# The first two blocks of each expert layer: early weights, rows chosen by 0/1 matrices, and a shift moved to VectorE, in a four-layer tower

## The chip, the cores and the metric

The kernel runs on 1 core of one Trainium2 chip, in float32. The metric is the device time of one execution in microseconds (us): the median of 3 runs.

## The reference, cut to what matters

Four layers run one after the other on 16 x 36 = 576 tokens of width 256. The change touches the mixtures of experts of layers 0, 2 and 3, called ffn0, ffn2 and ffn3 here. ffn0 sends each token to one of 8 experts, ffn2 to two of 8, ffn3 to two of 7.

```python
def _L0_ffn_ref(x, rms_w, gate_w, W1, b1, W2, b2):
    ms = jnp.mean(x * x, axis=-1, keepdims=True)
    xn = x * jax.lax.rsqrt(ms + EPS) * rms_w
    logits = jnp.einsum('btd,ed->bte', xn, gate_w)
    scores = jax.nn.softmax(logits, axis=-1)
    top1_idx = jnp.argmax(scores, axis=-1)
    top1_score = jnp.max(scores, axis=-1)
    out = jnp.zeros_like(xn)
    for e in range(E):
        h = jax.nn.silu(jnp.einsum('btd,df->btf', xn, W1[e]) + b1[e])
        ye = jnp.einsum('btf,fd->btd', h, W2[e]) + b2[e]
        out = jnp.where((top1_idx == e)[..., None], ye, out)
    return out * top1_score[..., None]
```

In ffn2 and ffn3 an expert is `silu(t @ a) * (t @ c) @ b`, the two chosen experts are summed with their weights, and one shared expert of the same form is added for every token. Between these stand recurrences (attn0, attn1, attn2, attn3) and a dense mixture (ffn1).

## The kernel before, in words

**An expert layer.** The normalized rows of the 576 tokens lie in `XH`, in five tiles of 128 tokens (the last has 64). TensorE transposes them, multiplies with the gate weights (`gate_logits`), VectorE finds the largest logits (`gates`), TensorE counts how many tokens each expert has ahead of each token (`ranks`), and VectorE turns that into a row number for each token (`places`). The rows of an expert fill whole blocks of 128 rows. The number of blocks is fixed, for the worst case: 12 in ffn0, 16 in ffn2, 15 in ffn3; `eid` says whose block each is. GpSimd scatters the rows of `XH` into the DRAM buffer `x_slots` (`dispatch`: 5 indirect DMAs in ffn0, 10 in ffn2 and ffn3). Then SyncE (SP) loads the blocks' rows and weights, TensorE multiplies, the result goes to `y_slots` in DRAM, and at the end GpSimd gathers it back per token (`collect`, with VectorE's `collect_tile`).

**The loop over blocks (`routed`).** Two weight buffers, each in two halves of about 1 MB. For block b, TensorE runs `up` of half 0, the `down` of half 1 of block b-1, the two transposes of the rows of block b+1, `up` of half 1, `down` of half 0. So a block is 24 products and 2 transposes in ffn0, 28 and 2 in ffn2 and ffn3. SP's program for block b (`emit` in `expert_blocks`) waits until the buffer's half is read (`downd`), and issues in this order: the rows of block b+2, half 0 of its weights, half 1, and then the finished rows of block b. All of these go through SP's one queue, in the order of the program.

**Which waits stand ahead of a layer.** SP waits for `eid_ready` before it loads any weights, and for all scatters (`scattered`) before it loads any rows.

**The shared expert** (`shared`) of ffn2 runs whole ahead of the blocks, in two halves of the tokens (384 and 192) with 3 steps each; that of ffn3 (6 steps per half) runs one half ahead of the blocks and one behind them. On VectorE, `weights` stands between `places` and `shared`.

**The shift b2 of ffn0** is added ahead of the blocks: TensorE transposes the gate weights `comb` and multiplies with `b20_s`, VectorE adds that to H (`side_tiles`). ScalarE copies each block's result to `y_s` (`y_copy`).

**keep_warm(n)** issues n turns of four bf16 products of 512 columns that nobody reads; `keep_warm(n, root=r)` then waits for a norm's variance and issues five more. They stand in TensorE's own order: what follows waits for them.

## Time and profile before

| | |
|---|---|
| runs | 862.98, 857.13, 854.99 us, median 857.13 |
| the profiled execution | 852.33 us, its span 850.5 us |
| TensorE busy | 768.8 us (90%) |
| mean granted TensorE clock | 0.979 |
| DMA moved | 139.45 MB, mean 164 GB/s |

All times in the rows further down are us from the start of that span. ffn0's blocks run from 121.34 to 212.5, ffn2's from 503.01 to 628.1, ffn3's from 711.08 to 829.5. In a timeline row, the first number is the start, the second the length; the bracket at its end is the idle time of that engine before it and what ended it. A float32 product shows as two records, so x48 is 24 products.

### The profile page before, as it was taken

To read this page: it belongs to the slowest core of one execution; us is meant where nothing else is said; L and a number is where in the kernel's file an instruction comes from. 1 tells how busy PE (TensorE), PEld (TensorE's weight loads), DVE (VectorE), ACT (ScalarE), POOL (GpSimd) and SP (SyncE) were. 2 spreads that over 40 slices of the span, in tenths; PEclk is the share of its full clock that TensorE was granted. 3 is DMA by queue.
4 is the path that set the end of the run, shared out by engine and by line. 5 is a ranking of instruction groups with operands and counts; after the bars stand their busy time and mean duration, and the time that the engine had idled before them with its cause. 6 is when DMAs were issued, how large, how long until landed. Compare 5 with 4: busy or idle time off the path is not lost.

```text
span 850.5 us, 12638 instructions
## 1 busy us (share of the span) xinstructions
PE 768.8 (90%) x4364; PEld 596.2 (70%) x4431; DVE 337.5 (40%) x949; ACT 254.6 (30%) x590; POOL 133.6 (16%) x101
## 2 busy tenths in 40 slices
PE   9999869999976679898988899999999989999996
PEld 6687449889543345674754579999965547999895
DVE  2215630000499957576758421111117731111113
ACT  1233124444353331563592222222210112222121
POOL 2000010000239940023050210000022040000004
PEclk9999889999999999999999799999999989999999
DMA  9700058996155502000000349999951062999962
GB/s 330 276 2 1 9 230 282 322 297 219 34 153 143 151 1 111 1 2 0 1 0 1 110 168 306 314 328 307 331 199 30 1 265 76 312 329 307 304 218 89
DMA packets 39842, 139.45 MB, mean 164 GB/s; under 512 B 5760, under 2 KB 20544, under 8 KB 28160
## 3 DMA queue, kind: packets, MB, share of 16 engines
q1 hardware_dynamic: 37568, 133.12, 46.7%
q0 software_dynamic: 2240, 5.90, 2.0%
q8 instruction: 18, 0.29, 0.2%
q14 instruction: 16, 0.13, 0.1%
HBM read 127.64 MB, written 11.35 MB: 163 GB/s over the span
## 4 chain that ended last, share of the span: by engine, by line
PE 59%; DVE 14%; issue 10%; DMA 8%; POOL 4%; ACT 3%; SPq 0%; DVEq 0%; POOLq 0%; ACTq 0%
PE PS L430 57%; DMA arena<-w_moe 4%; DVE arena L1680 4%; POOL arena L1281 2%; PE PS L487 1%; DVE stats L1362 1%; DMA arena<-x_slots 1%; PE PS L453 1%; DMA x_slots<-XH,posu 1%; DMA arena<-y_slots,posu 1%; POOL arena L1307 1%; DVE arena L1806 1%; DMA arena<-bc_scratch 1%; POOL arena L1294 1%; ACT XT L948 1%
## 5 line engine op out<-in xcount | busy, mean ns | idle before, releaser
L430 PE MATMUL PS<-arena 128*128 128x128 f32 (+4 forms) x2508 | 377.9, 310 | 12.1 <-DMA arena<-w_moe 3.1
L430 PEld LDWEIGHTS PS<-arena 128*128 128x128 f32 (+1 forms) x2508 | 334.7, 192 | 43.8 <-issue 13.4
L430 PE MATMUL PS<-warm 128*128 128x512 bf16 (+1 forms) x434 | 113.7, 379 | 7.8 <-DVE rs L1346 2.5
L1506 DVE TENSOR_TENSOR arena<-arena,PS 128x384 f32<-128x384 f32 (+1 forms) x62 | 30.2, 487 | 199.5 <-ACT arena L986 199.5
L430 PEld LDWEIGHTS PS<-warm 128*128 128x128 bf16 x501 | 49.7, 102 | 60.5 <-issue 7.1
L1281 POOL DMA_INDIRECT arena<-y_slots,posu x25 | 24.0, 961 | 381.7 <-DMA y_slots<-arena 375.0
L986 ACT ACTIVATE arena<-PS 128x384 f32<-128x384 f32 x62 | 30.4, 490 | 165.1 <-PE PS L430 165.1
L1294 POOL TENSOR_TENSOR arena<-arena 128x1152 f32<-128x1152 f32 x16 | 56.3, 3521 | 30.3 <-DVE arena L1680 30.3
L1518 DVE SCALAR_TENSOR_TENSOR H<-arena,wgt,H 128x256 f32<-128x256 f32 (+1 forms) x25 | 11.9, 477 | 120.6 <-DMA arena<-y_slots,posu 120.2
L430 PE MATMUL PS<-arena,ident 128*128 128x512 f32 (+1 forms) x128 | 38.0, 440 | 21.5 <-POOL arena L1294 21.5
L1270 POOL DMA_INDIRECT x_slots<-XH,posu x25 | 24.1, 964 | 172.5 <-DVE posu L1466 165.8
L430 PEld LDWEIGHTS PS<-arena,ident 128*128 128x128 f32 x128 | 20.5, 190 | 39.4 <-POOL arena L1294 24.1
L430 PE MATMUL PS<-XT,wsh 128*128 128x384 f32 (+1 forms) x144 | 43.5, 451 | 0.5 <-ACT arena L999 0.5
L1680 DVE TENSOR_TENSOR_SCAN arena<-PS,arena 128x576 f32<-128x576 f32 x32 | 41.6, 1340 | 0.0
L991 ACT ACTIVATE arena<-PS,arena 128x128 f32<-128x128 f32 x96 | 27.4, 367 | 43.1 <-PE PS L430 43.1
L430 PE MATMUL PS<-arena,wrnn_s 128*128 128x128 f32 (+1 forms) x280 | 36.7, 281 | 0.7
L430 PEld LDWEIGHTS PS<-arena,wrnn_s 128*128 128x128 f32 x280 | 33.8, 191 | 4.7 <-ACT arena L1052 3.9
L938 ACT ACTIVATE dev<-rs 128x5 f32<-128x5 f32 x19 | 4.1, 215 | 110.4 <-DVE rs L1346 110.4
L430 PEld LDWEIGHTS PS<-XT,wsh 128*128 128x128 f32 x144 | 28.0, 209 | 13.0 <-issue 5.5
L1113 ACT ACTIVATE PS<-arena 128x560 f32<-128x560 f32 x32 | 23.3, 731 | 35.5 <-DVE arena L1680 35.5
L430 PE MATMUL PS<-arena,wsh 128*128 128x384 f32 (+1 forms) x72 | 24.0, 460 | 9.7 <-DVE arena L1494 9.7
L999 ACT ACTIVATE arena<-PS 128x256 f32<-128x256 f32 x43 | 16.5, 383 | 38.5 <-PE PS L430 38.5
(262 smaller groups left out, 759.8 us busy)
## 6 DMA issues: line engine op xcount, KB each, us to landing
arena<-w_moe SPq DMA_DIRECT2D x31, 1152.0 KB, 6.5
arena<-w_moe SPq DMA_DIRECT2D x31, 1024.0 KB, 5.6
arena<-w_moe SPq DMA_DIRECT2D x24, 1026.0 KB, 6.1
arena<-bc_scratch SPq DMA_DIRECT2D x32, 288.0 KB, 3.8
arena<-x_slots SPq DMA_DIRECT2D x43, 128.0 KB, 2.5
y_slots<-arena SPq DMA_DIRECT2D x43, 128.0 KB, 5.2
wsh<-w_sh SPq DMA_DIRECT2D x1, 2176.0 KB, 8.5
wl_s<-w_l SPq DMA_DIRECT2D x1, 2048.0 KB, 13.1
```

Of the source, the lines that this page charges most:

```text
L430: return nc.tensor.matmul(out_, l, r, start=start, stop=stop, skip_group_check=True)
L453: last = nc.tensor.transpose(PS[:, j // 2, at:at + n_], XH[0:n_, j, 128 * d:128 * (d + 1)], ident[0:n_, 0:n_])
L986: nc.scalar.activation(sg_s[x][:, 0:3 * SB], PS[:, 2 * x, 0:3 * SB], ACT.Silu)\
L991: last = nc.scalar.activation(hid_b[x][:, SB * c:SB * (c + 1)], PS[:, 2 * x, SB * c:SB * (c + 1)], ACT.Silu, bias=wbuf[p][:, o_ + c:o_ + c ...
L999: nc.scalar.activation(y_s[p], PS[:, 4 + p, 0:D], ACT.Copy).then_inc(sem("y_sb"), 1)
L1113: nc.scalar.activation(inner(dA[d]), inner(dl[:, d, :]), ACT.Exp, scale=A_s[:, d, bass.ds(n, 1)])\
L1270: pool.indirect_dma_start(x_slots, bass.IndirectOffsetOnAxis(ap=posu[0:TILE_N[j], k, j:j + 1], axis=0), tile(XH, j), None).then_inc(sem("s ...
L1281: pool.indirect_dma_start(Yg[0:TILE_N[j], k, j * D:(j + 1) * D], None, y_slots[0:SB * NBLK[name], :], bass.IndirectOffsetOnAxis(ap=posu[0: ...
L1294: nc.gpsimd.tensor_tensor(hC[:, n % 2, :, :], hs_[:, n % 2, :, :], bcC[:, n:n + 1, :].to_broadcast([128, KD, T]), ALU.mult)\
L1506: ins = v.tensor_tensor(hid_b[x][:, 0:full], sg_s[x][:, 0:full], PS[:, 2 * x + 1, 0:full], ALU.mult)
L1518: link(v.scalar_tensor_tensor(tile(H, j), Yg[0:TILE_N[j], k, j * D:(j + 1) * D], wgt[0:TILE_N[j], k, j:j + 1], tile(H, j), ALU.mult, ALU.add))
L1680: v.tensor_tensor_scan(hs_[:, n % 2, d], dA[d], dBx[:, n % 2, d], 0.0, ALU.mult, ALU.add)\
```

## The change

1. **Blocks and experts.** Block e is the first 128 tokens of expert e; the blocks behind these hold what an expert has beyond 128. The numbers of blocks stay 12, 16 and 15. So blocks 0 and 1 always are experts 0 and 1, and SP issues their weights (`begin`) without `eid_ready`: in ffn0 when the products of the patches are done, in ffn2 and ffn3 when the recurrence ahead of them has read its last operands.
2. **Rows of blocks 0 and 1 in ffn0 and ffn2.** VectorE makes a 0/1 matrix per block (`chosen_rows`, five instructions of 128x128) and TensorE multiplies `XH` with it (`x_chosen`, ten products in place of a block's two transposes). In ffn3 the rows still come from `x_slots`.
3. **SP's order for block 0** in ffn0 and ffn2: half 0, half 1, then the wait for `scattered`, the rows of block 2, the finished rows.
4. **b2 of ffn0**: no products and no addition ahead of the blocks. SP loads the expert's row of b2 to 128 partitions for every block (`shift_in`), and VectorE adds it where ScalarE copied before (`shifted_rows`).
5. **gate_logits** multiplies the same eight gate columns twelve times over (96 columns), in all four layers that have gates; only the first eight are read.
6. **ffn2's shared expert**: one half ahead of the blocks, one behind them, as in ffn3. After it comes the same `keep_warm(21, root=18)`. The load of ffn3's shared weights now waits for it.
7. **VectorE's order** in ffn2 and ffn3: `places`, `shared`, `side_tiles`, then `weights`.
8. Four idle products ahead of the first `down` of the shared expert, seven ahead of attn1's last products.

```diff
@@ expert_blocks, on SP
-                def emit(b, hb, p, last=False):
+                def shift_in(e, p):
+                    if name == "ffn0":
+                        sp.dma_start(b2_s[p], b2_moe0[bass.ds(e, 1), :].to_broadcast([128, D])).then_inc(sem(f"b2{p}"), 16)
+
+                def emit(b, hb, p, last=False, first=False):
                     if not last:
                         e = expert_of(b + 2)
                         sp.wait_ge(sem("downd"), 2 * b + (2 * at + 1))
-                        rows_in(b + 2, p)
+                        if not first:
+                            rows_in(b + 2, p)
                         half(e, p, 0)
                         sp.wait_ge(sem("downd"), 2 * b + (2 * at + 2))
                         half(e, p, 1)
+                        if first:
+                            sp.wait_ge(sem("scattered"), 16 * SCAT[s])
+                            rows_in(b + 2, p)
                     rows_out(b, p)
-
-                sp.wait_ge(sem("eid_ready"), s + 1)
-                for b in range(2):
-                    e = expert_of(b)
-                    for x in range(2):
-                        half(e, b, x)
+                    if not last:
+                        shift_in(e, p)
+
+                def begin():
+                    for b in range(2):
+                        for x in range(2):
+                            half(b, b, x)
+                        shift_in(b, b)
@@ gate_logits, on TensorE
-                        last = mm(PS[0:TT, 3, E * j:E * (j + 1)], XT[:, k, TT * j:TT * (j + 1)],
-                                  gatew[:, GATES[name], k, :], k == 0, k == KD - 1)
+                        last = mm(PS[0:TT, 3, LG * j:LG * (j + 1)].rearrange("p (r e) -> p r e", e=E),
+                                  XT[:, k, TT * j:TT * (j + 1)],
+                                  gatew[:, GATES[name], k, None, :].to_broadcast([128, LG // E, E]), k == 0, k == KD - 1)
@@ routed, on TensorE
+                def x_chosen(b):
+
+                    pe.wait_ge(sem("one_hot"), 2 * ONE_HOT.index(name) + b + 1)
+                    for d in range(KD):
+                        for j in range(NT):
+                            last = mm(PS[:, 7 - b, SB * d:SB * (d + 1)], tile(XH, j)[:, 128 * d:128 * (d + 1)],
+                                      one_hot[b][0:TILE_N[j], j, :], j == 0, j == NT - 1)
                     last.then_inc(sem("xt_t"), 1)
@@ TensorE's program
+            idle_products(7)
             pe.wait_ge(sem("ys_ready"), 1)
@@
-            shared("ffn2", [128] * CS, ranked=True)
+            shared("ffn2", [128] * CS, (0,), ranked=True)
             routed("ffn2")
+            pe.wait_ge(sem("y_sb"), BLK0["ffn2"] + NBLK["ffn2"] + 2)
+            shared("ffn2", [128] * CS, (1,))
 
 
             keep_warm(21, root=18)
@@ VectorE
+            def chosen_rows(name, b):
+
+                if b == 0:
+                    dve.wait_ge(sem("xt_t"), BLK0[name]) if BLK0[name] else None
+                for j in range(NT):
+                    ins = v.tensor_scalar(one_hot[b][0:TILE_N[j], j, :], tri[0:TILE_N[j], 4, :], cnt[0:TILE_N[j], b, j:j + 1],
+                                          mks[0:TILE_N[j], b, j:j + 1], ALU.is_equal, ALU.mult)
+            def shifted_rows(b, hb, p):
+                dve.wait_ge(sem("downd"), 2 * b + 2)
+                dve.wait_ge(sem(f"y{p}"), 16 * hb + 16)
+                dve.wait_ge(sem(f"b2{p}"), 16 * hb + 16)
+                v.tensor_tensor(y_s[p], PS[:, 4 + p, 0:D], b2_s[p], ALU.add).then_inc(sem("y_sb"), 1)
```

How this moves instructions, at three places. The first is SP's program around block 0 of ffn0. `w_moe` are weights, `x_slots` the rows in, `y_slots` the rows out, `b_moe` the row of b2. Before, from the rows of blocks 0 and 1 to the end of `emit` for block 0:

```order
L359 DMA arena<-x_slots 128x256 x2
L350 TENSOR_LOAD eid
L350 ISA x2
L359 DMA arena<-x_slots 128x256
L356 ISA
L356 DMA arena<-w_moe 128x2052
L356 ISA
L356 DMA arena<-w_moe 128x2052
L363 DMA y_slots<-arena 128x256
```

Now, the same `emit`:

```order
L361 ISA
L361 DMA arena<-w_moe 128x2052
L361 ISA
L361 DMA arena<-w_moe 128x2052
L364 DMA arena<-x_slots 128x256
L368 DMA y_slots<-arena 128x256
L372 ISA
L372 DMA arena<-b_moe 128x256
```

The rows of block 2 have moved from ahead of its two halves of weights to behind both, and a load of b2 has come in behind the finished rows.

The second is TensorE's program in ffn0 from the ranks to the first products of block 0. `warm` are idle products, `ident,comb` and `b_s,combT` the shift, `ident,arena` the transposes of a block's rows. Before:

```order
L439 UNCONDITIONAL_BRANCH
L430 MATMUL PS<-warm 128x512 x4
L439 REGISTER_ALU
L439 COMPARE_AND_BRANCH
L707 MATMUL PS<-ident,comb 8x128 x4
L707 MATMUL PS<-ident,comb 8x64
L430 MATMUL PS<-b_s,combT 128x256 x4
L430 MATMUL PS<-b_s,combT 64x256
L439 UNCONDITIONAL_BRANCH
L430 MATMUL PS<-warm 128x512 x4
L439 REGISTER_ALU
L439 COMPARE_AND_BRANCH
L487 MATMUL PS<-ident,arena 128x128 x2
L430 MATMUL PS<-arena 128x128 x8
L487 MATMUL PS<-ident,arena 128x128 x2
L430 MATMUL PS<-arena 128x128 x8
```

Now (`arena,XH` are the products with the 0/1 matrices):

```order
L478 UNCONDITIONAL_BRANCH
L469 MATMUL PS<-warm 128x512 x4
L478 REGISTER_ALU
L478 COMPARE_AND_BRANCH
L469 MATMUL PS<-arena,XH 128x128 x10
L469 MATMUL PS<-arena 128x128 x8
L469 MATMUL PS<-arena,XH 128x128 x10
L469 MATMUL PS<-arena 128x128 x8
L469 MATMUL PS<-arena 128x256 x4
```

The shift and its idle products are gone, the three turns of idle products behind the ranks have stayed, and ten products stand where two transposes stood, twice.

The third is TensorE's program at the end of ffn2's blocks. Before:

```order
L430 MATMUL PS<-arena 128x128 x12
L430 MATMUL PS<-arena 128x256 x3
L430 MATMUL PS<-arena 128x128 x10
L430 MATMUL PS<-arena 128x256 x6
L439 UNCONDITIONAL_BRANCH
L430 MATMUL PS<-warm 128x512 x4
```

Now (`XT,wsh` and `arena,wsh` are the shared expert, `ident,YT` the transposes of its result):

```order
L469 MATMUL PS<-arena 128x128 x12
L469 MATMUL PS<-arena 128x256 x3
L469 MATMUL PS<-arena 128x128 x10
L469 MATMUL PS<-arena 128x256 x6
L469 MATMUL PS<-XT,wsh 128x192 x8
L469 MATMUL PS<-arena,wsh 128x192 x2
L469 MATMUL PS<-XT,wsh 128x192 x4
L469 MATMUL PS<-arena,wsh 128x192 x4
L604 MATMUL PS<-ident,YT 128x128 x2
L604 MATMUL PS<-ident,YT 64x128 x2
L478 UNCONDITIONAL_BRANCH
L469 MATMUL PS<-warm 128x512 x4
```

The second half of the shared expert stands between the last block and the 21 turns of idle products (L439 before, L478 now), which are the same.

## Rows read from the trace of the kernel before

**Rows 1.** The page, part 4: shares of the chain that ended last, by engine.
```profile
PE 59%; DVE 14%; issue 10%; DMA 8%; POOL 4%; ACT 3%; SPq 0%; DVEq 0%; POOLq 0%; ACTq 0%
```

**Rows 2.** The chain of waits around ffn0's start: start, length, what.
```profile
109.81 6.80 DMA x_slots<-XH,posu
116.62 3.18 DMA arena<-x_slots
121.34 3.75 PE PS L430 x16
```

**Rows 3.** Timeline of PE in ffn0: ranks, first transposes, one block.
```profile
99.54 1.45 PE L430 MATMUL PS<-mks,tri 128*128 128x40 f32 x6
...
119.85 0.69 PE L487 MATMUL PS<-ident,arena 128*128 128x128 f32 x2 [5.14 <-DMA arena<-x_slots]
...
132.51 7.19 PE L430 MATMUL PS<-arena 128*128 128x128 f32 x48
```

**Rows 4.** Timeline of DVE: a 128x128 instruction; places and weights in ffn2.
```profile
227.18 0.47 DVE L1632 TENSOR_SCALAR arena<-ident,colv 128x128 f32<-128x128 f32 x2
...
478.41 0.20 DVE L1437 COPY cnt<-PS 128x40 f32<-128x40 f32 x1 [2.48 <-PE PS L430]
...
481.77 0.23 DVE L1417 TENSOR_TENSOR gk<-mks,ge 128x40 f32<-128x40 f32 x1
...
483.86 1.02 DVE L1494 TENSOR_TENSOR arena<-arena,PS 128x384 f32<-128x384 f32 x2
```

**Rows 5.** Stretches: PE, PEld, DVE, ACT, POOL busy, granted clock, DMA share, GB/s.
```profile
97.10:99.50 2.40, 2.40 (x9) 0.71 (x6) 2.13 (x20) 0.52 (x1) 0.00 (x0) 0.66 0.01 3
101.00:105.30 4.30, 3.64 (x9) 1.53 (x11) 3.76 (x21) 0.00 (x0) 0.76 (x1) 0.57 0.00 0
121.30:125.20 3.90, 3.86 (x18) 3.89 (x19) 0.00 (x0) 1.26 (x2) 0.00 (x0) 0.50 0.00 0
473.30:477.60 4.30, 4.30 (x10) 2.42 (x10) 2.29 (x21) 1.52 (x2) 0.00 (x0) 0.60 0.00 0
487.20:491.40 4.20, 4.20 (x10) 2.29 (x9) 0.00 (x0) 0.00 (x0) 3.18 (x4) 0.62 1.02 426
```

**Rows 6.** More stretches, same columns: a block, attn1's end, ffn1's logits, ffn3.
```profile
146.80:154.00 7.20, 7.20 (x51) 6.69 (x50) 0.00 (x0) 3.18 (x11) 0.00 (x0) 1.00 0.98 334
205.00:212.00 7.00, 7.00 (x44) 6.43 (x44) 0.00 (x0) 2.67 (x9) 0.00 (x0) 1.00 0.09 28
312.20:318.60 6.40, 6.40 (x21) 4.62 (x22) 2.99 (x7) 0.00 (x0) 0.00 (x0) 0.73 0.00 0
333.00:340.40 7.40, 7.33 (x46) 6.43 (x47) 4.49 (x30) 1.53 (x3) 0.00 (x0) 1.00 0.00 1
677.10:681.40 4.30, 4.30 (x11) 2.38 (x11) 2.29 (x21) 1.52 (x2) 0.00 (x0) 0.62 0.00 0
```

**Rows 7.** SP's DMAs to y_slots, 132.9 to 134: block 0's, from issue to landing.
```profile
DMA to landing us min/median/max: 5.5/5.5/5.5
```

**Rows 8.** The page, part 6: DMA issues, size, median us to landing.
```profile
arena<-x_slots SPq DMA_DIRECT2D x43, 128.0 KB, 2.5
```

**Rows 9.** Timeline of PE in ffn2: wait, first block, last turns, next transposes.
```profile
484.47 2.93 PE L430 MATMUL PS<-arena,wsh 128*128 128x384 f32 x4 [3.41 <-DVE arena L1494]
...
503.01 2.92 PE L430 MATMUL PS<-arena 128*128 128x128 f32 x24 [0.56 <-ACT arena L975]
...
628.17 18.08 PE L430 MATMUL PS<-warm 128*128 128x512 bf16 x63
...
648.73 0.44 PE L453 MATMUL PS<-ident,XH 128*128 128x128 f32 x2 [0.27 <-DVE XH L1372]
```

**Rows 10.** Timeline of PE in ffn3: the wait, and the shared half at the end.
```profile
688.30 2.87 PE L430 MATMUL PS<-arena,wsh 128*128 128x384 f32 x4 [3.41 <-DVE arena L1494]
...
710.13 0.38 PE L487 MATMUL PS<-ident,arena 128*128 128x128 f32 x2
...
829.93 2.87 PE L430 MATMUL PS<-XT,wsh 128*128 128x192 f32 x16 [0.47 <-ACT arena L999]
```

## What the change does to the time, predicted

> **What bounds the kernel now.** I read the chain of waits first: TensorE carries 59% of it, and what is left comes in pieces between long runs of products [rows 1]. So a change pays only where TensorE waits, or where it works at the lower of its two clocks. I then went through the timeline of TensorE around the three layers of blocks, through VectorE's timeline for what it waits for there, and through a table of stretches for the granted clock and the DMA share.
>
> In ffn0 the end of the start-up is set by a path through memory. The last scatter lands 6.80 us after its start at 109.81, the rows take 3.18 us more, and the first products of block 0 start at 121.34 [rows 2]. TensorE has idled 5.14 us by then, and the clock is 0.50, so 1.2 GHz, up to 125.2 [rows 3, 5]. After that TensorE works without a break: 24 products, 4096 columns, in 7.19 us [rows 3], some 1.7 ns a column (128 columns 0.213 us), with a DMA share of 0.98 beside it [rows 6]. So in the blocks TensorE and the transfers are near a tie.
>
> In ffn2 and ffn3 the shared expert covers the scatter. What stands open is the 3.41 us in which TensorE waits for VectorE (`places`, then `weights`) [rows 4, 9, 10], and half clock ahead of it and behind it: 0.60 and 0.62 in ffn2, 0.62 in ffn3 [rows 5, 6].
>
> **The change part by part.** Sums are made against the profiled execution (852.33 us, 4.8 below the median 857.13), and the difference is carried over to the median.
>
> *a. ffn0, start.* Ranks start at 99.54 as now, as they wait for VectorE. They took 1.45 us at half clock; I take 0.73, the wide logits having kept the clock (c). Counts and offsets to the first 0/1 matrix are about six small steps of 0.2 us; the matrix is five instructions of 128x128 at 0.235 us or less [rows 4], about 1.1 us: ready at 102.6. The three turns of idle products, still ahead in TensorE's order, end at about 102.9. Ten products of 0.213 us give 105.0, ScalarE's copy 0.8: first product at 105.85 and not 121.34. **-15.5.** Weights are long there.
>
> *b. ffn0, block 1's rows* in ten products and not two transposes: eight more of 0.213. **+1.7.** Its matrix, made behind `places`, is ready at about 106, and TensorE asks at 107.5.
>
> *c. ffn0, block 2's rows.* Now SP issues them behind `downd` of block 0's second half, which falls inside block 1, and TensorE wants them right after that same `down`. Nothing hides the transfer, and it stands behind half 1 of the weights in the queue. The nearest row is the store of block 0's result, issued in just that place behind the same half: 5.5 us to landing [rows 7]. With 0.45 us for SP's two issues, TensorE waits **+5.95**. Behind this wait `up`, `down` and all later blocks queue. Bounds: 2.5 us, the median of such rows with little ahead of them [rows 8], and 6.80 [rows 2]. Half clock follows such a wait, but it stood at the start before [rows 5], so in ffn0 it cancels.
>
> *d. ffn0, b2.* Ten more loads of 128 rows of 1 KB in the blocks. While only stores ran, at 205 to 212, 28 GB/s over 7 us (196 KB) took 0.09 of the DMA's time, 0.63 us, so 0.42 us for 131 KB [rows 6]. The other bound is what a block has left: 0.98 x 7.2 = 7.06 us busy, of which 2.1 MB of weights at 426 GB/s [rows 5] are 4.9, so 1.05 us for each of the two row transfers. At 0.42 a block comes to 7.48 against TensorE's 7.25, at 1.05 to 8.1. I take the low end, since rows out have the same size and form, and 0.15 a block of its 0.23, since a share counts packets in flight and not only room taken: **+1.5** for ten blocks; range 0 to 8.5. ("DMA: Bandwidth & Descriptors" of the Trainium skill, Specifications, gives about 358 GB/s from HBM for a core; 2.49 MB a block would take 6.96 us by it, and the sum would be 1.5 lower. The 426 of the row is above that figure.) VectorE's addition itself is hidden: ScalarE did it before, and VectorE is idle in the blocks.
>
> *e. attn1's end.* The stretch had clock 0.73 over 6.4 us, 3.5 us of it at half [rows 6]. Seven idle products (1.5 us) fill the 1.7 us gap: **-1.5**. Bounds 0 and -1.75.
>
> *f. ffn2, start.* With full clock `up` ends at 476.0 (it ran at 0.60, +1.6), ranks and the second `up` at 479.3, idle products at 480.2. `places` took 3.36 us from 478.41 to 481.77, then `weights` 2.1 to 483.86 [rows 4]; now `places` is about 0.35 longer, two matrices (2.1) take the place of `weights`, so the first `down` is at 483.25, not 484.47. The idle time is 3.05 us against 3.41: I take the half clock behind it, about 6 us long, as it was. The first half's products (6.4 us at full clock, 9.4 so), the copy and transposes (1.6), ten products (2.1) and a copy (0.6) give 496.9, not 503.01. **-6.1.** The second half is what has left.
>
> *g. ffn2, blocks.* As b and c: +1.7 and +5.95. Here the clock was full at the start (503.01: 24 records in 2.92 us [rows 9]), so the half clock behind the wait is new: about 4.6 us of work at half, +2.3. **+9.95.**
>
> *h. ffn2, end.* The last block ends at 628.14. Before, 21 turns took 18.08 us at once, and the transposes of attn3 came at 648.73, 20.6 us behind, timed by the gather [rows 9]. Now the shared half comes first: start after 0.47 us [rows 10], 18 products of 192 columns (5.8), a wait of 0.25 for the last `down`, copy and transposes 1.3: 7.9 us. Then the same 18.08 and the five products (1.1): 27.1 us behind the last block. The rows of XH are ready earlier, so what is late next is TensorE's own idle work. **+6.5.** It is exposed in full; below it lies only VectorE's later `collect`, which would take over at about 24 us.
>
> *i. ffn3.* Full clock in `up` (-1.6 by itself), `weights` gone from the path (2.1 less 0.35): first `down` at 684.9 and not 688.30, with 1.0 us of idle time, so I take no half clock behind it (1.7 saved; the stretch behind was 0.52 and 0.85 in the mean). Transposes of block 0 at 704.5, not 710.13 [rows 10]. Scatters start 1.5 us earlier and land with the queue empty; rows are there at 703.3. **-5.6.** SP's order in its blocks is the old one: nothing there.
>
> The wide logits cost nothing: 96 columns are 0.16 us at full clock, and a product of 8 columns already took 0.24.
>
> Sum: -15.5 + 1.7 + 5.95 + 1.5 - 1.5 - 6.1 + 9.95 + 6.5 - 5.6 = **-3.1 us**: 849.2 for the profiled execution, **854.0** for the median.
>
> **The rivals.**
>
> *The waits for block 2's rows are short.* If transfers overlap in the queue and rows land in 2.5 us, c and g lose 3.0 each, and with a wait of 3 us in ffn2 the 2.3 of half clock may go: -8.3, 845.7, faster by over 1%. Against it stands the one row in exactly this place [rows 7]. Chance 0.15.
>
> *The clock doesn't follow the wide logits* (slower than before). The drop to 0.66 and 0.57 in ffn0 and 0.60 in ffn2 came behind the narrow logits [rows 5]; but ffn1 has the same logits, and its stretch 333.0 to 340.4 is at 1.00 [rows 6], so the logits alone don't decide it. If the clock falls all the same, a loses about 3.0 (idle turns at half clock stand ahead of `x_chosen`), f and i 1.6 each, e 1.5: +7.7, 861.7. From 3.1 us of such loss on the change is a loss. Chance 0.15. ("TensorE: Matmul & The Clock Gate" of the Trainium skill, Part 1, says that activity releases the throttle; by it denser logits help everywhere, and the sum stands as it is.)
>
> *b2 makes the transfers the bound in ffn0.* At 1.05 us a load, +7.0 over d: 861.0. For it: share 0.98 already. Against: stores of that size took 0.42 us. Chance 0.08.
>
> *The idle turns of h are hidden.* Were the gather later than 27 us, h would be 0 and the time 847.5. The gather is 20.6 us behind now, and the shared weights' load that moves into it costs a few us. Chance 0.04.
>
> **How the numbers follow.** The forecast has 0.58. The range takes in the short waits (845.7 less small terms) and the clock (861.7 and some of b2): 844.5 to 863.5. A measurement of this kernel tells about 1% from no change. Faster by over 1% (below 848.6): the short waits, the hidden turns, and a little of the forecast's own spread, 0.22. Slower by over 1% (above 865.7): two of the slow cases at once, or b2 at its upper end with one more miss, 0.12. Within 1%: 0.66.
>
> **What would show it.** Right: first product of block 0 in ffn0 near 106; an idle time near 6 us in TensorE inside block 1 of ffn0 and of ffn2, released by `x_slots`, with clock 0.50 behind it; idle products running on for 6 to 7 us after VectorE's last XH at the end of ffn2, without a wait of TensorE there; block 0's transposes in ffn3 at 5 to 6 us less behind their logits. Wrong: waits for `w_moe` in most blocks of ffn0 (b2), a clock near 0.6 behind the logits (a, f, i), or no half clock behind ffn2's wait of 3.05 us, which would give 3.0 more.

## The result, and the profile after

| | before | after |
|---|---|---|
| median, 18 runs each | 855.19 us | 861.03 us |
| ratio | | 1.0072, 95% interval 1.0052 to 1.0091 |
| the profiled execution, its span | 850.5 us | 858.3 us |
| TensorE busy | 768.8 us | 771.9 us (90%) |
| mean granted clock | 0.979 | 0.986 |
| DMA moved | 139.45 MB | 140.44 MB |

The change makes the kernel about 6 us, 0.7%, slower. I had forecast 3.1 us less. The time lies inside the range, but on the other side of no change. One of the 18 runs after took 1018.81 us at a granted clock of 0.747, where the others had 0.979 to 0.987; the ratio is taken without it. The mean clock of the profiled execution is better than before, and still time was lost: the larger part went to waits for transfers.

The page of after, part 4, the chain that ended last (the first row is comparable with [rows 1]; `L469` is the helper that was `L430`):

```profile
PE 65%; DVE 13%; DMA 8%; issue 7%; POOL 3%; ACT 3%; SPq 1%; another core or an unknown queue 0%; DVEq 0%; POOLq 0%; ACTq 0%
PE PS L469 62%; DMA arena<-x_slots 3%; DVE arena L1765 3%; DMA arena<-w_moe 3%; DMA arena<-bc_scratch 2%; POOL arena L1342 1%; PE PS L527 1%; DVE stats L1410 1%; PE PS L492 1%; POOL arena L1355 1%; DVE arena L1891 1%; ACT XT L999 1%; DVE H L1636 0%; DVE TMP L1632 0%
```

`x_slots` (rows in) and `w_moe` (weights) now carry 3% each of the chain. Where this is spent is seen in TensorE's timeline. After, ffn0 (start, length, instructions; in brackets the idle time ahead and its releaser):

```profile
99.36 0.84 PE L469 MATMUL PS<-mks,tri 128*128 128x40 f32 x6 [0.67 <-DVE mks L1454]
...
102.77 3.08 PE L469 MATMUL PS<-arena,XH 128*128 128x128 f32 x20
106.66 2.02 PE L469 MATMUL PS<-arena 128*128 128x128 f32 x16 [0.81 <-ACT arena L1025]
108.52 2.98 PE L469 MATMUL PS<-arena,XH 128*128 128x128 f32 x20
111.42 7.29 PE L469 MATMUL PS<-arena 128*128 128x128 f32 x48
125.00 0.69 PE L527 MATMUL PS<-ident,arena 128*128 128x128 f32 x2 [6.28 <-DMA arena<-x_slots]
125.48 8.50 PE L469 MATMUL PS<-arena 128*128 128x128 f32 x48
...
145.54 3.78 PE L469 MATMUL PS<-arena 128*128 128x128 f32 x24 [0.58 <-DMA arena<-w_moe]
...
158.42 0.44 PE L527 MATMUL PS<-ident,arena 128*128 128x128 f32 x2 [1.39 <-DMA arena<-x_slots]
...
170.95 3.77 PE L469 MATMUL PS<-arena 128*128 128x128 f32 x24 [1.32 <-DMA arena<-w_moe]
...
183.94 0.44 PE L527 MATMUL PS<-ident,arena 128*128 128x128 f32 x2 [1.97 <-DMA arena<-x_slots]
```

The first product of block 0 starts at 106.66, where it was 121.34 [rows 2]. Then come 6.28 us of idle time for block 2's rows, and behind that shorter waits, up to 2.0 us each, in most blocks, for weights and rows in turn. After, ffn2, same columns:

```profile
482.17 1.95 PE L469 MATMUL PS<-arena,wsh 128*128 128x384 f32 x4 [3.75 <-DVE arena L1568]
...
495.94 2.92 PE L469 MATMUL PS<-arena 128*128 128x128 f32 x24 [0.56 <-ACT arena L1021]
...
515.46 0.69 PE L527 MATMUL PS<-ident,arena 128*128 128x128 f32 x2 [6.10 <-DMA arena<-x_slots]
...
639.60 19.37 PE L469 MATMUL PS<-warm 128*128 128x512 bf16 x89
658.81 0.38 PE L492 MATMUL PS<-ident,XH 128*128 128x128 f32 x2
```

The same kind of wait stands at 515.46, and at the end the 21 turns of idle products and the five behind them run for 19.4 us, with no idle time of TensorE ahead of the transposes. After, the stretches that answer [rows 5] and [rows 6] (busy us of PE, PEld, DVE, ACT, POOL; granted clock, DMA share, GB/s):

```profile
97.10:99.50 2.40, 1.73 (x10) 0.65 (x8) 2.03 (x20) 0.24 (x1) 0.00 (x0) 1.00 0.00 0
101.00:105.30 4.30, 4.30 (x27) 2.83 (x25) 3.92 (x22) 0.00 (x0) 0.00 (x0) 1.00 0.00 0
125.00:133.80 8.80, 8.80 (x50) 8.36 (x51) 0.00 (x0) 2.90 (x10) 0.00 (x0) 0.82 0.23 63
473.00:477.60 4.60, 4.60 (x19) 2.65 (x18) 3.29 (x21) 2.01 (x4) 0.00 (x0) 1.00 0.22 87
482.10:491.40 9.30, 8.61 (x20) 4.45 (x20) 1.03 (x3) 1.07 (x2) 7.16 (x8) 0.82 0.29 99
515.40:525.70 10.30, 10.24 (x58) 9.86 (x59) 1.24 (x3) 1.36 (x3) 0.00 (x0) 0.74 0.22 56
```

Behind the logits the clock is 1.00 now, where it was 0.66, 0.57 and 0.60. Behind the waits of 6.28, 3.75 and 6.10 us it is 0.82, 0.82 and 0.74 in the mean, so part of each stretch is at 1.2 GHz.

From marks that both timelines have, the ledger is as follows. Each mark is the start of the work named. What a stage gained or lost is the difference between its end mark and its start mark, after less before.

| mark | before | after | shift | stage |
|---|---|---|---|---|
| ffn0, first product of block 0 | 121.34 | 106.66 | -14.7 | -14.7 |
| idle products behind ffn0's last block | 212.56 | 211.96 | -0.6 | +14.1 |
| idle products behind attn1's last products | 318.55 | 316.45 | -2.1 | -1.5 |
| ffn2, logits | 471.03 | 469.02 | -2.0 | 0.1 |
| ffn2, first product of block 0 | 503.01 | 495.94 | -7.1 | -5.1 |
| ffn2, end of the last block | 628.14 | 631.46 | +3.3 | +10.4 |
| attn3, transposes | 648.73 | 658.81 | +10.1 | +6.8 |
| ffn3, first product of block 0 | 711.08 | 716.27 | +5.2 | -4.9 |
| end of the span | 850.5 | 858.3 | +7.8 | +2.6 |

### The profile page after: what moved, and what is told of

The parts are those of the page before. It is cut to its first block, busy times and chain, and to the rows that moved or that the text cites. A ratio compares the mean times of both kernels' runs of the same rounds, so it can differ in the third digit from the quotient of the medians.

```text
span 858.3 us, 12832 instructions
## 1 busy us (share of the span) xinstructions
PE 771.9 (90%) x4479; PEld 599.8 (70%) x4479; DVE 348.1 (41%) x991; ACT 250.6 (29%) x576; POOL 133.2 (16%) x101
## 2 busy tenths in 40 slices
DMA packets 40850, 140.44 MB, mean 164 GB/s; under 512 B 5872, under 2 KB 21552, under 8 KB 29168
## 4 chain that ended last, share of the span: by engine, by line
PE 65%; DVE 13%; DMA 8%; issue 7%; POOL 3%; ACT 3%; SPq 1%; another core or an unknown queue 0%; DVEq 0%; POOLq 0%; ACTq 0%
PE PS L469 62%; DMA arena<-x_slots 3%; DVE arena L1765 3%; DMA arena<-w_moe 3%; DMA arena<-bc_scratch 2%; POOL arena L1342 1%; PE PS L527 1%; DVE stats L1410 1%; PE PS L492 1%; POOL arena L1355 1%; DVE arena L1891 1%; ACT XT L999 1%; DVE H L1636 0%; DVE TMP L1632 0%
## 5 line engine op out<-in xcount | busy, mean ns | idle before, releaser
L469 PE MATMUL PS<-arena 128*128 128x128 f32 (+4 forms) x2508 | 379.4, 311 | 11.8 <-DVE arena L1894 3.1
L469 PEld LDWEIGHTS PS<-arena 128*128 128x128 f32 (+1 forms) x2508 | 337.0, 193 | 42.9 <-issue 11.6
L469 PE MATMUL PS<-warm 128*128 128x512 bf16 (+1 forms) x492 | 116.6, 374 | 2.8 <-DVE rs L1394 1.5
L469 PEld LDWEIGHTS PS<-warm 128*128 128x128 bf16 x492 | 48.4, 101 | 56.0 <-issue 4.2
L469 PE MATMUL PS<-arena,ident 128*128 128x512 f32 (+1 forms) x128 | 38.0, 440 | 21.5 <-POOL arena L1342 21.5
L1318 POOL DMA_INDIRECT x_slots<-XH,posu x25 | 24.2, 966 | 178.9 <-DVE posu L1537 172.2
L469 PEld LDWEIGHTS PS<-arena,ident 128*128 128x128 f32 x128 | 20.5, 190 | 39.3 <-POOL arena L1342 24.0
L1702 DVE TENSOR_TENSOR arena<-PS,arena 128x256 f32<-128x256 f32 x12 | 5.1, 425 | 92.7 <-PE PS L469 92.7
L469 PE MATMUL PS<-XT,wsh 128*128 128x384 f32 (+1 forms) x144 | 39.3, 420 | 0.9 <-ACT arena L1045 0.9
L469 PEld LDWEIGHTS PS<-arena,wrnn_s 128*128 128x128 f32 x280 | 33.8, 191 | 4.7 <-ACT arena L1099 3.9
L469 PE MATMUL PS<-arena,wrnn_s 128*128 128x128 f32 (+1 forms) x280 | 36.7, 281 | 0.0
L469 PEld LDWEIGHTS PS<-XT,wsh 128*128 128x128 f32 x144 | 26.0, 196 | 11.1 <-ACT arena L1045 1.8
L469 PE MATMUL PS<-arena,wsh 128*128 128x384 f32 (+1 forms) x72 | 22.3, 436 | 9.9 <-DVE arena L1568 9.4
L527 PE MATMUL PS<-ident,arena 128*128 128x128 f32 x78 | 15.8, 285 | 16.3 <-DMA arena<-x_slots 16.3
```

What stands on the lines that cost most here:

```text
L469: return nc.tensor.matmul(out_, l, r, start=start, stop=stop, skip_group_check=True)
L527: last = nc.tensor.transpose(PS[:, 7 - p, SB * d:SB * (d + 1)], xslot[p][:, 128 * d:128 * (d + 1)], ident[:, :])
L1318: pool.indirect_dma_start(x_slots, bass.IndirectOffsetOnAxis(ap=posu[0:TILE_N[j], k, j:j + 1], axis=0), tile(XH, j), None).then_inc(sem("s ...
```

## The experiments

Four kernels at a time ran on one chip, beside the kernel before. Ratios are to the kernel before on that chip; the changed kernel is 1.0072 in the result and 1.008 (1.0049 to 1.0111) when it ran again in the third group, and the kernel with eight harmless instructions more, which serves as the changed kernel in the second, is 1.0089.

**Block 2's rows ahead of the halves.** In ffn0 and ffn2, SP waits for `scattered` and issues the rows of block 2 before both halves of weights and not behind them.

```diff
-                        if not first:
-                            rows_in(b + 2, p)
+                        if first:
+                            sp.wait_ge(sem("scattered"), 16 * SCAT[s])
+                        rows_in(b + 2, p)
                         half(e, p, 0)
                         sp.wait_ge(sem("downd"), 2 * b + (2 * at + 2))
                         half(e, p, 1)
-                        if first:
-                            sp.wait_ge(sem("scattered"), 16 * SCAT[s])
-                            rows_in(b + 2, p)
```

> The changed kernel, with the wait for the scatters and the rows of block 2 ahead of its two halves of weights, as for all other blocks. If the order on the SP queue alone makes the two waits of 6.3 and 6.1 us, both go (the scatters have landed by then), with the half clock behind them (1.3 and 2.3 us): 16 us less, about 845. If the waits are the scatters themselves, or if TensorE then runs into the DMA limit that the waits gave it time for, they shrink by less than half, or the gain is under 8 us.

Measured: 845.84 us, ratio 0.9892 (0.9867 to 0.9916), about 15 us below the changed kernel and faster than before. TensorE's timeline of this kernel at block 2 of ffn0:

```profile
111.37 7.29 PE L467 MATMUL PS<-arena 128*128 128x128 f32 x48
118.50 0.38 PE L525 MATMUL PS<-ident,arena 128*128 128x128 f32 x2
118.72 7.19 PE L467 MATMUL PS<-arena 128*128 128x128 f32 x48
```

No wait, and the block takes 7.19 us and not 8.50. SP's timeline says why, first of the changed kernel, then of this one:

```profile
115.39 3.84 SPq L361 DMA_DIRECT2D arena<-w_moe  x2
119.28 0.42 SPq L364 DMA_DIRECT2D arena<-x_slots  x1
```

```profile
115.18 0.34 SPq L364 DMA_DIRECT2D arena<-x_slots  x1
115.72 3.44 SPq L361 DMA_DIRECT2D arena<-w_moe  x2
```

The same 128 KB took 5.7 us to landing when they were issued at 119.28, behind half 1, and 2.1 us at 115.18, ahead of it. The wait for `scattered`, ahead of it in this kernel, ended at 113.1, 2 us before the rows were issued, and held nothing up. In ffn2 it is the same: this kernel's transposes for block 2 have no idle time ahead of them, and the block behind takes 7.67 us, where the changed kernel waits 6.10 us and then takes 9.97.

```profile
502.31 0.38 PE L525 MATMUL PS<-ident,arena 128*128 128x128 f32 x2
502.53 7.67 PE L467 MATMUL PS<-arena 128*128 128x128 f32 x56
```

So both waits, and the half clock behind them, come from the place in SP's program alone. ("DMA: Bandwidth & Descriptors" of the Trainium skill, in "Two DMAs through the same engine are not ordered", says that within one queue of one DMA engine descriptors start in order, though they need not end so. That fits these two numbers: the small transfer starts behind the megabyte that was issued right ahead of it.)

**ffn0 without b2's loads in the blocks.** VectorE's wait for these loads goes with them.

```diff
                     rows_out(b, p)
-                    if not last:
-                        shift_in(e, p)
```

> The changed kernel without the ten loads of b2 inside ffn0's blocks (only the first two remain, so every block adds the rows of experts 0 and 1: this part of the computation is left out). If those loads are what makes TensorE wait in ffn0's blocks 3 to 11, the stretch from its first product of block 0 to its last shrinks from 105.3 us to about 99 and the kernel comes to about 855, with rows landing in 2.5 us and not 4.3. If the waits come from elsewhere (weights of more different experts, or the late start of the stream behind block 2's wait), the stretch stays within 1.5 us of 105.3 and the kernel at 859 to 861.

Measured: 858.12 us, ratio 1.0048 (1.0017 to 1.0079). TensorE's timeline from block 3 on shows no wait for a transfer: six blocks take 43.6 us (142.15 to 185.74), 7.26 us each, where the changed kernel takes 50.2 (141.06 to 191.24), 8.36 each. The stretch 142 to 198 of the changed kernel, then of this one:

```profile
142.00:198.00 56.00, 50.33 (x340) 45.34 (x339) 2.55 (x6) 19.29 (x68) 0.00 (x0) 1.00 0.91 303
```

```profile
142.00:198.00 56.00, 56.00 (x389) 51.91 (x388) 3.39 (x8) 22.16 (x76) 0.00 (x0) 1.00 0.97 327
```

and their DMAs in it, in the same order (size, median us to landing):

```profile
arena<-w_moe SPq DMA_DIRECT2D x13, 1026.0 KB, 7.3
y_slots<-arena SPq DMA_DIRECT2D x7, 128.0 KB, 7.0
arena<-b_moe SPq DMA_DIRECT2D x7, 128.0 KB, 6.8
arena<-x_slots SPq DMA_DIRECT2D x7, 128.0 KB, 4.4
```

```profile
arena<-w_moe SPq DMA_DIRECT2D x15, 1026.0 KB, 5.7
y_slots<-arena SPq DMA_DIRECT2D x8, 128.0 KB, 5.3
arena<-x_slots SPq DMA_DIRECT2D x7, 128.0 KB, 2.3
```

With b2 every transfer lands 1.6 to 2.1 us later, and TensorE loses 5.7 us of 56. Without it TensorE is busy throughout and the DMA still moves more per second. From first to last product ffn0 takes 98.1 us and not 105.3. Other traces with the changed kernel's ffn0 have 103.6 to 105.9, and 48.4 to 50.2 for the six blocks. The stop for block 2's rows is there with b2 and without it (6.28 and 6.11 us), and it does not make the later waits: the kernel with block 2's rows first has no such stop and still took 47.4 us for the six blocks. So b2 costs 5.5 to 7.8 us in the traces, in the upper half of my range of 0 to 8.5. The ratios of the two kernels differ by 2 to 3 us only, from different chips and with an interval of 2.6 us each side for the kernel without b2; its profile has 8.7 us of another wait at its end, discussed below.

**What of b2 costs: its bytes, its packets, or its one row?** Three kernels. In the first, b2 lies in the weight record of half 1 (the same bytes, no transfer of its own; finished rows go ahead of half 1, since VectorE reads b2 out of the weight buffer):

```diff
-        b2_s = [take(D) for _ in range(2)]
+        b2_s = [wbuf[p][:, sum(HLEN["ffn0"]) - D:sum(HLEN["ffn0"])] for p in range(2)]
...
-                        sp.wait_ge(sem("downd"), 2 * b + (2 * at + 2))
+                        if name == "ffn0":
+                            rows_out(b, p)
+                        else:
+                            sp.wait_ge(sem("downd"), 2 * b + (2 * at + 2))
                         half(e, p, 1)
```

> The changed kernel, but in ffn0 b2 lies in the weight record of half 1 (256 more columns of it, the same bytes in all) and has no transfer of its own; finished rows are therefore issued ahead of half 1. Theory O (the small loads cost by themselves, as packets of 1 KB of one row in a full queue): the waits of ffn0 for w_moe and x_slots inside the blocks go almost entirely, first to last product 98 to 100 us instead of 105.3, and the time is 855 to 857. Theory Y (the bytes cost: 131 KB more a block on transfers that are at their bound): 131 KB at 334 GB/s are 0.39 us a block, and TensorE's block has 7.25 us against 7.5: first to last product 102 us or more, 858 to 860. If issuing rows ahead of half 1 holds half 1 up, waits for w_moe of half 1 grow.

In the second, b2 is read from 128 separate rows (SP's load names them instead of repeating one):

```diff
-    a["b2_moe0"] = x["L0_ffn_b2"]
+    a["b2_moe0"] = np.ascontiguousarray(np.broadcast_to(x["L0_ffn_b2"][:, None, :], (E, 128, D)))
```

> The changed kernel, but b2 is loaded from 128 separate rows in memory (written out on the host as copies) and not from one row 128 times. Number, size and place of the loads are the same. Theory R (128 reads of the same row collide in memory, which is what makes the load dear): ffn0's waits fall as without b2, 98 to 100 us from first to last product instead of 105.3, time 855. Theory O or Y (packets or bytes, wherever they come from): as the changed kernel, 104 to 106 us and 861.

In the third, each load in the blocks brings 8 of the 256 columns:

```diff
                     if not last:
-                        shift_in(e, p)
+                        shift_in(e, p, 8)
```

> The changed kernel, but each load of b2 inside the blocks brings 8 columns of the 256 (the other columns of b2 are left as they came at the start, so those experts' shift is wrong for them): as many loads, as many packets, 4 KB instead of 131 KB. Six blocks took 50.2 us with b2, 47.7 with the same bytes inside the weight record, 43.6 without b2. Theory O (what is left beside the bytes is the separate load with its 128 small packets): six blocks take 46 us or more, and the time is 857 to 859. Theory Y (bytes, and the stalls that follow from them, as each wait of TensorE also delays SP's next issue): six blocks take 43.6 to 44.3 us and the time is 853 to 855.

| kernel | us, ratio | six blocks of ffn0 from block 3 | first to last product |
|---|---|---|---|
| no b2 in the blocks | 858.12, 1.0048 | 43.6 | 98.1 |
| 4 KB a load | 854.92, 1.0025 (0.9995 to 1.0055) | 45.0 | 101.2 |
| in the record | 857.22, 1.0065 (1.0035 to 1.0096) | 47.7 | 104.9 |
| the changed kernel | 861.03, 1.0072 | 50.2 (48.8 when run again) | 105.3 (104.5) |
| 128 rows | 860.31, 1.0104 (1.0056 to 1.0152) | 48.5 | 103.9 |

The source rows don't matter: that theory fell. The bytes matter most: against the changed kernel run again on the same chip (858.30, six blocks 48.8), 4 KB a load in place of 131 saves 3.7 us over six blocks and 3.4 us of the time. The 45.0 us lie between what the two theories on record had asked for (43.6 to 44.3, and 46 or more). What is left with small loads, 1.5 us over six blocks, is about what the load costs by itself, as far as one trace of each kernel can tell. In the record the bytes cost nearly as much: 47.7 us for the six blocks is 0.7 below the lowest trace of the changed order, the 104.9 us from first to last product are far from the 98 to 100 that packets as the cause would give, and the gain in the whole, 2 to 3 us against its neighbours of 859.08 and 860.31, is inside what the intervals leave open. But 131 KB at the 327 GB/s that the stage moves without b2 are 0.40 us a block, and the blocks lose 0.7 (record) to 0.8 to 1.1 us (own load). The rate sinks as well, to 317 and 303 GB/s over 142 to 198, with the DMA share at 0.90 and 0.91 and not 0.97. The reading that fits: SP may only issue the next half when TensorE has finished with the buffer, so every wait of TensorE delays the next issue and leaves the DMA engines a gap. The rows show the waits and the lower share; that one makes the other I have argued, not shown.

**The wide logits.** Eight columns and not 96:

```diff
-LG = 12 * E
+LG = E
```

> The changed kernel with the old gate logits of 8 columns. If the wide logits hold the clock in ffn0, ffn2 and ffn3, the granted clock falls back to about 0.6 behind the logits in all three and the kernel is 3 to 6 us slower, 864 to 867. If the clock was held by something else in the change, the clock stays at 1.00 and the time at 861.

Measured: 867.45 us, ratio 1.0144 (1.0111 to 1.0177), about 6 us above the changed kernel. The stretches of this kernel that answer the table above:

```profile
97.00:99.50 2.50, 2.50 (x8) 0.86 (x7) 2.13 (x20) 0.24 (x1) 0.00 (x0) 0.54 0.00 0
101.00:105.30 4.30, 4.30 (x24) 2.46 (x23) 3.93 (x21) 0.00 (x0) 0.00 (x0) 1.00 0.00 0
473.00:477.60 4.60, 4.60 (x15) 2.69 (x14) 2.08 (x20) 1.98 (x3) 0.00 (x0) 0.67 0.50 208
688.50:693.00 4.50, 4.40 (x24) 3.54 (x25) 1.82 (x19) 1.54 (x3) 0.00 (x0) 0.79 1.02 431
```

With eight columns the clock falls behind the logits, to 0.54, 0.67 and 0.79 in these stretches. It costs 0.7 us from ffn0's logits to its first product (12.82 and not 12.14), 1.5 us in ffn2 (14.63 from the logits to the first `down` and not 13.15) and 1.5 in ffn3 (11.79 and not 10.31). That is 3.7 of the 6; the others I have not found. The wide logits themselves cost 0.07 us a layer (2.47 and not 2.40).

**ffn2's end.** First 12 turns of idle products and not 21, alone:

```diff
-            keep_warm(21, root=18)
+            keep_warm(12, root=18)
```

> The changed kernel with 12 turns of idle products and not 21 behind ffn2's shared half. If TensorE's own idle work sets the start of attn3 (6.8 us late), the turns end 7.7 us earlier and the transposes then wait for VectorE: 3 to 6.5 us less, about 856, the rest being VectorE's gather, which the load of the shared weights now falls into. If the gather were the bound anyway, nothing changes (861).

Measured: 861.46 us, ratio 1.0074 (1.0043 to 1.0105), no gain that can be measured. Its trace shows where the gain stopped. TensorE behind the last block (ends at 634.2), then VectorE:

```profile
642.34 10.52 PE L469 MATMUL PS<-warm 128*128 128x512 bf16 x48
656.30 2.32 PE L469 MATMUL PS<-warm 128*128 128x512 bf16 x5 [3.44 <-DVE rs L1394]
658.41 0.63 PE L492 MATMUL PS<-ident,XH 128*128 128x128 f32 x2
```

```profile
641.17 0.48 DVE L1592 SCALAR_TENSOR_TENSOR H<-arena,wgt,H 128x256 f32<-128x256 f32 x1 [0.48 <-DMA arena<-y_slots,posu]
...
648.46 0.48 DVE L1592 SCALAR_TENSOR_TENSOR H<-arena,wgt,H 128x256 f32<-128x256 f32 x1 [5.55 <-DMA arena<-y_slots,posu]
```

The transposes come 24.2 us behind the last block and not 27.35, and VectorE had stood 5.55 us over one gathered row, right behind the issue of ffn3's 2 MB of shared weights at 641.30. Locally 3 us were gained, in this one trace; why the median doesn't show them stays open. The held row was there in the changed kernel too (VectorE's timeline of after):

```profile
645.87 0.48 DVE L1592 SCALAR_TENSOR_TENSOR H<-arena,wgt,H 128x256 f32<-128x256 f32 x1 [5.65 <-DMA arena<-y_slots,posu]
...
654.88 1.70 DVE L1420 TENSOR_SCALAR XH<-H,mv,rs 128x256 f32<-128x256 f32 x5
```

Its last XH ends at 656.58, 2.2 us before the idle products do, so fewer turns alone could give little. Then the same with that load moved behind the gather:

```diff
+            sp.wait_ge(sem("var_ready"), 18)
             load(wsh[:, :], w_sh3, "sh3")
```

> The changed kernel with 12 turns of idle products at ffn2's end and not 21, and ffn3's shared weights loaded only once the last statistics of ffn2's collect are there, so behind the gather. With 12 turns alone VectorE waited 5.55 us for gathered rows at 648.46, right behind the issue of that load. Theory G (the load of 2 MB holds up the gather's rows, and this is what now bounds ffn2's end once the turns are fewer): the wait of 5.6 us falls below 1.5, transposes of attn3 follow the last block's end by 20.5 to 21.5 us instead of 27.35 in the changed kernel and 24.2 with 12 turns alone, the time is 854 to 856. Rival (the gather is slow by its own issue on GpSimd, 1.25 us each for ten, whatever moves beside it): 23.5 to 24.5 us behind the last block and a time of 858 to 861.

Measured: 851.52 us, ratio 1.0008 (0.9982 to 1.0034), 7.6 us below its neighbour on the chip with the changed order (859.08). VectorE waits at most 0.85 us for a gathered row, the load is issued at 651.40, and TensorE's timeline shows the transposes 20.1 us behind the last block (632.81):

```profile
640.95 11.68 PE L470 MATMUL PS<-warm 128*128 128x512 bf16 x53
652.90 0.44 PE L493 MATMUL PS<-ident,XH 128*128 128x128 f32 x2 [0.27 <-DVE XH L1421]
```

So in the changed kernel the idle turns set ffn2's end, and right behind them stood the gather, held up by a transfer that nobody waits for until 687.

**ScalarE's wait in the tail.** The change took eight instructions out of ScalarE's program. In the profile after, ffn3's last shared half has a wait that names no semaphore of this core (ScalarE's timeline):

```profile
846.53 0.33 ACT L1073 ACTIVATE arena<-PS 128x192 f32<-128x192 f32 x1 [4.74 <-PE PS L469]
850.81 0.33 ACT L1073 ACTIVATE arena<-PS 128x192 f32<-128x192 f32 x1 [3.95 <-remote]
```

```diff
+            for _ in range(8):
+                nc.scalar.activation(pad_c[:, _:_ + 1], col("gamma"), ACT.Exp)
```

> The changed kernel with eight more instructions at the start of ScalarE's program (eight 128x1 activations into a tile that nobody reads, while ScalarE waits there anyway); the change had taken eight instructions out of ScalarE's program (428 before, 420 after). Theory F (the wait of 4.0 us of ScalarE ahead of a silu of ffn3's last shared half, with no semaphore as its releaser and one instruction transfer beside it, is code that comes late, and where that falls depends on the number of instructions ahead): the instruction transfer in the tail moves out of the shared half, the wait of 4.0 us goes, and the kernel takes 3 to 5 us less, 856 to 858 where the changed kernel has 861. Rival (the wait is one for another transfer or for the profiler, and stands for the work done there): wait and time unchanged, 861.

Measured: 859.08 us, ratio 1.0089 (1.0058 to 1.012). The wait is gone, but so it is in the three kernels beside it, without the eight instructions, and the time is the same. The changed kernel once more, in the third group:

> The changed kernel as it is, once more, beside the three others on one chip, so that they are compared with it and not only with the kernel before. The four traces of the last chip show no wait of ScalarE without a semaphore in ffn3's last shared half, with eight instructions more or without, while the five traces before them all do (4 to 9 us). Theory S (the wait belongs to some chips or executions, since the same code has it and has it not): it may be there or not, and the times of the two chips differ by no 4 us against the kernel before; ratio 1.007 to 1.009, 860 us. Theory T (it is a steady part of the changed kernel's time): it is there, and the ratio is the same.

Measured: 858.30 us, ratio 1.0080 (1.0049 to 1.0111); no such wait in its trace. ffn3 from block 0's first product to the start of the last transposes takes 134.3 us in it (716.82 to 851.15) and took 134.8 before (711.08 to 845.90). So the number of instructions does not make the wait. Five traces have it, with 4 to 9 us (after, and the four kernels of the first chip); the eight of the other two chips and that of the kernel before don't. What it is stays open. The +2.6 in the ledger's last line is this wait; the changed kernel loses about as much against the kernel before where its trace has the wait (5.8 us) as where it hasn't (6.2), so the wait does not explain the result.

**The repairs together.** Rows of block 2 first, 12 turns, shared weights behind the gather; and the same with b2 in the record.

> The two repairs together: block 2's rows issued ahead of the halves (15 us alone, from 861 to 846), and 12 idle turns with ffn3's shared weights behind the gather (7.6 us alone, from 859 to 851.5). Theory A (the two places are independent): the sum of the two, 22 to 24 us below the changed kernel, 836 to 839. Rival (ffn2's end is set by the gather whose start moves with the blocks, so part is paid twice): 840 to 844.

> The same two repairs, and b2 in the weight record of half 1 with finished rows of ffn0 issued ahead of it. Theory A: b2 in the record gave 2 to 3 us on the changed kernel, where six blocks fell from 50.2 to 47.7 us; here too, 834 to 837. Rival (without the stop for block 2's rows the queue is fuller at the start of ffn0, and half 1 lands late since finished rows go ahead of it): no gain over the same without the record, 837 to 840, with more waits for w_moe.

Measured: 835.36 us, ratio 0.9800 (0.9749 to 0.9851), and 834.26 us, ratio 0.9803 (0.9755 to 0.9852). The two repairs add up: 22.9 us below the changed kernel on that chip (858.30), where 15 and 7.6 were found singly. The record adds nothing that can be measured. Both beat the kernel before by 2%, by the intervals 1.5 to 2.5%, and the first differs from the changed kernel in a handful of lines.

## Why the prediction was wrong, step by step

The signs were all as forecast, and so were most mechanisms; nearly every term came out somewhat dearer, or gained somewhat less, than forecast. The largest miss, and the one whose mechanism I had held unlikely, is b2.

- **a. ffn0's start**, -15.5 forecast, -14.7 measured. The clock held (1.00 at 101 to 105.3). The miss is the price of the products: 20 records in 3.08 us are 0.31 us a product and not 0.213. That figure was a little low even for the blocks (4096 columns in 7.19 us are 0.22 for 128), and I had taken it over from long runs of other products.
- **b. Block 1's rows**, +1.7 forecast. From start to start the rows give 2.90 us for the ten products and 0.37 for two transposes: +2.5. Same cause.
- **c. Block 2's rows in ffn0**, +5.95 forecast, 6.28 measured. The nearest row, a store in the same place, was the right one. The half clock cancelled as forecast: the block behind the wait lost 1.6 us (8.82 from its transposes to the next, and not 7.24), and block 0's first products gained 1.7 (16 records in 2.02 us and not 3.75). In some other traces the products of the block behind the wait took up to 1.3 us more than here, 9.8 us and not 8.5.
- **d. b2**, +1.5 forecast with 0 to 8.5 as bounds. 5.5 to 7.8 against the kernel without it, +5.1 in the ledger against the kernel before. This step failed. I had two prices, 0.42 and 1.05 us a load, and took the low one, times a factor of 0.65. The blocks lost 0.8 to 1.1 us each. The low price came from a stretch where little else was moving (share 0.09), which says nothing of a queue at 0.98. I gave "b2 makes the transfers the bound" a chance of 0.08, with the share of 0.98 written beside it. Its premise was a misreading as well: I wrote that TensorE works without a break in the blocks of the kernel before. It does not. Its six blocks took 45.8 us, where 43.6 is clean, with waits such as this one (its timeline):

```profile
165.99 3.77 PE L430 MATMUL PS<-arena 128*128 128x128 f32 x24 [0.81 <-DMA arena<-w_moe]
```

So the transfers were already the later ones at times, and little in ffn0 was left to hide a new load. The stage of +14.1 in the ledger adds up: block 0's clock -1.7, b +2.5, c +6.3, the clock behind c +1.6, the later blocks +5.1, and 0.3 that is spread.
- **e. attn1's end**, -1.5 forecast, -1.5 measured.
- **f. ffn2's start**, -6.1 forecast, -5.1 measured (-4.0 when the kernel ran again; the half clock behind the wait was longer there). TensorE waited 3.75 us for VectorE and not 3.05: the ten instructions of the two matrices took 2.83 us and not 2.1.

```profile
478.69 2.83 DVE L1484 TENSOR_SCALAR arena<-tri,cnt,mks 128x128 f32<-128x128 f32 x10
```

- **g. ffn2's blocks**, +9.95 forecast, +10.4 measured: a wait of 6.10 us, clock 0.74 behind it. Wait and block 1's products make 9.05, the half clock 2.6, and 1.2 came back in later blocks, where the kernel before had short waits.
- **h. ffn2's end**, +6.5 forecast, +6.8 measured. The sign that I had named, idle products running on for 6 to 7 us behind VectorE's last XH, was 2.2 us: the size came out, but the gather was nearly as late as the turns. I had written that below it lay only VectorE's collect, at about 24 us. With 12 turns it took over at 24.2. I had taken that for the gather's own length; it was the load of the shared weights beside it, and without that the figure is 20.1.
- **i. ffn3's start**, -5.6 forecast, -4.9 measured.
- **The tail**, nothing forecast, +2.6 in this one profile, from a wait of unknown cause that came and went.

The ledger's stages, less the tail, sum to +5.2, close to the 5.8 us between the medians, and 8.3 above my -3.1. Of these 8.3, b2 is 3.6 by the ledger; the rest is small misses, nearly all the same way. With b2 alone put right the forecast would have been a loss of 0.5 us by the ledger's price, and 0.9 to 3.2 by that against the kernel without it. With all the others put right and b2 left, it would have been a loss of 1.6. So either was enough to turn the sign, and that the time fell inside my range is no credit to the sum.

Of the rivals, the short waits did not occur as the kernel stood (5.7 us to landing); the clock followed the wide logits, which were worth 6 us, near my price of 7.7 for its failing; the hidden turns did not occur; b2 as the bound did, at 5.5 to 7.8 us where the rival had 8.5.

## What to carry to other kernels

Where TensorE and the transfers are near a tie, price added bytes by what the stage has left, at the stage's own rate, and expect more than that: here 131 KB were 0.40 us of bytes and cost 0.7 to 1.1. A price from a quiet stretch is no guide, and short waits for transfers in the trace say that the tie is already lost. When code is reordered so that a wait moves, look at what is now issued ahead of it: a small transfer that is wanted soon must not stand behind a megabyte in the same queue. When a wait is covered by idle work of fixed length, shorten both together, and ask which transfers beside the next wait could come later.

## What the runs showed of the hardware that I had not expected

- The same 128 KB row transfer landed in 2.1 us when issued ahead of 1 MB of weights, and in 5.7 us behind it, in the same queue.
- Over 56 us of weights, rows in and rows out, this core moved 327 GB/s at a DMA share of 0.97 (without b2, 142 to 198), although stretches of 4 us show 426 and 431 GB/s. ("Perfetto Trace Analysis" of the Trainium skill, "Roofline", gives about 435 GB/s of the 16 DMA engines as the bound of a single core. The short stretches agree with it; the long one stayed well below.)
- Gate logits of 96 columns cost 0.07 us more than of 8, and hold the granted clock at 1.00 where it fell to 0.54.
- Products with the 0/1 matrices, groups of five over the token tiles, took 0.31 and 0.30 us for 128 columns, where 128 columns were 0.22 us in the blocks [rows 3].
- A wait of ScalarE of 4 us was there in one execution and not in another of the same code, at a cost in the profiled time but none that the medians show. On record I had an instruction transfer beside it; the nearest one in that trace lies at 838 to 839, and the wait begins at 846.9.
